# Picked rows of the second attention group through two PSUM banks in turn

## Chip, cores and metric

One core of one Trainium2 chip. The metric is device time in microseconds of one execution; before, three runs gave a median of 261.88 us (261.1 to 262.32).

## What is computed

Two blocks run one after the other on x of shape (2, 512, 128), both steered by a row of conditions. The first (quantised linear layers with a gated scan over time) is untouched and done before the stretch in question. The second begins with attention, 16 heads of width 8 over 512 positions:

```
xn = layernorm(x, g1, be1)
xm = xn * (1 + sc_a) + sh_a
qkv = xm @ Wqkv
scores = (q @ k.T) * 8 ** -0.5, causal
x = x + gt_a * (softmax(scores) @ v @ Wproj + bproj)
```

An MLP with its own normalisation follows.

## The kernel before, in words

The kernel is written engine by engine: five programs in a fixed order (PE, ACT, DVE, POOL, SP) that wait for each other by semaphores. PSUM is one tensor of eight banks, 128 by 512 fp32 each, called bank(0) to bank(7).

**Parts.** The scores are computed in bf16 from operands split into three bf16 parts. For each batch b and side i (0 for queries, 1 for keys) ACT writes `part[b][i][0]` (L739, a copy out of PSUM), DVE the remainder `rest` (L1216), ACT `part[b][i][1]` (L745), DVE `part[b][i][2]` (L1222, in `split_last`). The parts then go into stacks QS and KS, in which the six useful products of parts stand under each other.

**Stacks by DMA or by picking.** Attention runs in eight groups of four heads, four groups to a batch. Most heads are stacked by DMA: SP issues those of QS, POOL those of KS (`stack_parts`, L327). The first two groups of the first batch don't wait for DMAs: PE multiplies selection matrices (`picks`) with the three parts, which puts the stacked rows into a bank (`pick`, L1454, three matmuls with 512 columns), and ACT copies the bank into QS (L730) or KS (L732), in `picked`. The semaphore `picked_pe` counts the picks that PE has done, `picked_act` the copies of ACT. The first group is picked ahead of the attention into banks 4 to 7. The second group has four picks, low and side in turn: QS, KS, QS, KS. All four go through bank 6 and stand between the score items of the first group.

**Score items.** `S_ITEMS` cuts a group into 12 items by query tile and head, 256 to 512 columns wide. For each, PE makes three products (L1513 to L1515: scores and causal masks) in one of the banks 4, 5, 7 in turn, and DVE takes the row maximum (L1241). An item may start when DVE has read the item three before it (`bank_free`). After item 3 of the next group PE transposes the maxima (L1525), once POOL has split them into three bf16 parts (`split_maxima`, L474 to L480, which waits for all 12 items of its group). ACT copies them (L777), SP sends them into QS (L358), and PE computes the scores again for the exponentials, transposed and with the maxima as extra rows (`exp_slot`, L1553 to L1559, first behind item 7 of the second group). ACT takes the exponentials (L763), PE multiplies with V (L1573).

**Orders written out by hand around the change.** PE: projections of the second batch (L1463, L1469), items 0 to 2 of the first group, pick one, items 3 and 4, pick two, items 5 and 6, pick three, items 7 and 8, pick four, items 9 to 11, then the second group, whose first item waits for all six picked copies. Before each of the four picks PE waits until ACT has copied the previous one. ACT: part 0 of the second batch (L739), part 1 of it (L745, waits for DVE's remainders), the copy of V (L751), the four picked copies, then the maxima and exponentials. DVE: items 0 and 1, the remainders of the second batch (L1216, `split_rest`), items 2 to 5, its last parts (L1222, `split_last`), items 6 to 11 and on. POOL: the KS transfers of the second batch (ten for parts 0 and 1, two for part 2), two additions of a bias (L466), the splits of the maxima.

Of the kernel before, what the change touches and what calls it, by code (L numbers as in the profile page):

```python
# [84 lines left out]
NG = H // HG  # L85
HH = H // 2
PICKED = 2
HP = 2 * PICKED


# [51 lines left out]
def build(nc, x, cond_w, wa4, cond_rows, main_w, l1_w, bcast_rows, cols, rows1, consts, out):  # L142
    with ExitStack() as ctx:
# [43 lines left out]
        attn = [sb(f"attn{b}", [P, NT, D]) for b in range(B)]  # L187
        picks = sb("picks", [P, 2, 3, HP, P], BF16)

# [65 lines left out]
        S = {n: ctx.enter_context(nc.semaphore(n)) for n in SEMAPHORES}  # L255
# [62 lines left out]
        def stack_parts(queue, b, i, wanted=range(3)):  # L318

            stack, parts, done = ((QS[b], Q_PART, q_stacked[b]), (KS[b], K_PART, k_stacked[b]))[i]  # L320
            skip = HP if b == 0 else 0
            for want in wanted:
# [172 lines left out]
        def _(act):  # L495
# [146 lines left out]
            for i, parts in enumerate((Q_PART, K_PART)):  # L642
                for p in range(3):
                    slots = [s for s, q in enumerate(parts) if q == p]
                    step = slots[1] - slots[0] if len(slots) > 1 else 1
                    for half in range(2):
                        dst = picks[:, i, p, :, half * ROWS:(half + 1) * ROWS].rearrange("c h (s d) -> c h s d", d=HD)
                        src = ident_b[:, half * ROWS:half * ROWS + HP * HD].rearrange("c (d h) -> c h d", h=HP)
                        nc.scalar.activation(dst[:, :, slots[0]:slots[-1] + 1:step, :],
# [19 lines left out]
            def centre(b, n, done):  # L669

                act.wait_ge(S["ln_bias"], n)
                for t in range(b * NT, b * NT + NT):
                    ins = nc.scalar.activation(xhat[:, t, :], xs[:, t, :], ACT.Identity, bias=nbias[:, t:t + 1],  # L673
                                               scale=rstd[:, t:t + 1])
                ins.then_inc(done, 1)
# [50 lines left out]
            def picked(g, low, i, n, bk):  # L726

                act.wait_ge(S["picked_pe"], n)
                if i == 0:
                    ins = nc.scalar.activation(QS[0][:, slot_head(g, low), :], bank(bk), ACT.Copy)  # L730
                else:
                    ins = nc.scalar.activation(KS[0][:, slot_head(g, low), :], bank(bk), ACT.Identity,  # L732
                                               bias=k_f[:, KC["kone"][0]:KC["kone"][1]])
                ins.then_inc(S["picked_act"], 1)

            for b in range(B):
                for i in range(2):
                    act.wait_ge(S["qk_pe"], 2 * b + i + 1)
                    nc.scalar.activation(part[b][i][0][:, :], bank(2 + i), ACT.Copy,  # L739
                                         scale=QK_SCALE[i]).then_inc(S["part0"], 1)  # L740
                if b == 0:
                    centre(1, B + 1, S["xhat_ready"])
                for i in range(2):
                    act.wait_ge(S["rest_ready"], 2 * b + i + 1)
                    nc.scalar.activation(part[b][i][1][:, :], rest[b][i][:, :], ACT.Copy).then_inc(S["part1"], 1)  # L745
                if b == 0:
                    modulate_columns(1, 0)
                    picked(0, 0, 0, 1, 4)
                    picked(0, 1, 0, 3, 6)
                act.wait_ge(S["v_pe"], b + 1)  # L750
                nc.scalar.activation(V1[b][:, :, :, 0:HD].rearrange("p t h d -> p (t h) d"),  # L751
                                     bank(0).rearrange("p (n d) -> p n d", d=HD), ACT.Copy
                                     ).then_inc(S["v_ready"], 1)
            for n in range(4):
                low, i = divmod(n, 2)
                picked(1, low, i, 4 + n + 1, 6)

            def exp_slot(n, s):
                if s == 0 and n >= 2:
# [529 lines left out]
        def _(pe):  # L1289
# [45 lines left out]
            for i, j in enumerate((0, 1, 3, 4)):  # L1335
                ins = T.matmul(bank(4)[:, 16 + B * i:16 + B * (i + 1)], lw[:, a + j * D:a + (j + 1) * D], scT[:, :],
                               start=True, stop=True)
# [6 lines left out]
            for b in range(B):  # L1344
                ins = T.matmul(bank(4)[:, b:b + 1], crow[:, a + b * P:a + (b + 1) * P], cs_of(4, 7),
                               start=True, stop=True)
# [4 lines left out]
            for b in range(B):  # L1351
                for a in range(0, OUT6, 512):
                    z = min(a + 512, OUT6)
                    for c in range(OC):
                        ins = T.matmul(bank(2 * b + a // 512)[:, 0:z - a], cxq[:, c, b:b + 1].to_broadcast([P, P]),
                                       w4q[:, c, a:z], start=(c == 0), stop=(c == OC - 1))
# [4 lines left out]
            for i, j in enumerate((2, 5)):  # L1361
                for b in range(B):
# [3 lines left out]
                    ins = T.matmul(dst, ones[0:1, :], row1[:, g0 + i * D:g0 + (i + 1) * D], start=False, stop=True)  # L1366
# [44 lines left out]
            for t in range(NT):  # L1411
                for b in range(B):
# [5 lines left out]
                    for j in range(2):  # L1418
                        ins = T.matmul(bank(4 * b + 2 * (t % 2) + j), xq3[b][:, 1, tok(t)],
                                       weights("wm1")[:, j * MLP:(j + 1) * MLP], start=True, stop=True)  # L1420
# [30 lines left out]
            def pick(g, low, i, p, bk):  # L1451

                pe.wait_ge((S["part0"], S["part1"], S["part2"])[p], i + 1)
                return T.matmul(bank(bk), picks[:, i, p, slot_head(g, low), :], part[0][i][p][:, :],  # L1454
                                start=(p == 0), stop=(p == 2))
# [40 lines left out]
            def score_item(n, i):  # L1496
# [5 lines left out]
                bank_free(k)  # L1502
                if i == 0 and n < PICKED:
                    pe.wait_ge(S["picked_act"], (2, 6)[n])
# [30 lines left out]
            def exp_slot(n, s):  # L1535

                b, g = divmod(n, NG)
                use = 5 * n + s
                if use == 0:
                    pe.wait_ge(S["rest_ready"], 2 * B)  # L1540
                    pe.wait_ge(S["v_ready"], B)
                    pe.wait_ge(S["v_ones"], B)
                if s == 0:
                    pe.wait_ge(nm_stacked[n % 2], 32 * (n // 2 + 1))
                if use >= 2:
                    pe.wait_ge(S["p_ready"], use - 1)
                pairs = {0: [(0, 0)], 1: [(1, 0)], 2: [(0, 1), (0, 3)], 3: [(1, 1), (1, 3)], 4: [(0, 2), (1, 2)]}[s]
                for low, kt in pairs:
                    dsts = [bank(2 * (use % 2) + half)[:, p_at(2 * half + low, kt)[1] % L:][:, 0:L - kt * P] for half in range(2)]
                    h = slot_head(g, low)  # L1550
                    for half in range(2):
                        rows = half_rows(2 * half, XROWS)
                        T.matmul(dsts[half], KS[b][rows, h, tok(kt)], QS[b][rows, h, kt * P:L], start=True, stop=False)  # L1553
                    for half in range(2):
                        r = half_rows(2 * half)
                        T.matmul(dsts[half][:, 0:P // 2], k_of("pickLo", r), k_of("maskKlo", r), start=False, stop=False)  # L1556
                    for half in range(2):
                        r = half_rows(2 * half)
                        ins = T.matmul(dsts[half][:, 0:P], k_of("pickHi", r), k_of("maskKhi", r), start=False, stop=True)  # L1559
                ins.then_inc(S["st_pe"], 1)  # L1560
# [53 lines left out]
            for n in range(N_GROUPS + 3):  # L1614
                for i in range(len(S_ITEMS)):
                    if n < N_GROUPS:
                        score_item(n, i)
                    if n == 0 and i in (2, 4, 6, 8):
                        low, side = divmod(i // 2 - 1, 2)
                        pe.wait_ge(S["picked_act"], 2 + i // 2 - 1)  # L1620
                        for p in range(3):
                            ins = pick(1, low, side, p, 6)
                        ins.then_inc(S["picked_pe"], 1)
                    if i == MAXIMA_AT and 1 <= n <= N_GROUPS:
                        maxima(n - 1)
                    if i == MAXIMA_AT and n >= 3:
                        values_rows(n - 3)
                    if i in E_OLD and 2 <= n <= N_GROUPS + 1:
                        exp_slot(n - 2, E_OLD[i])
                    if i in E_NEW and 1 <= n <= N_GROUPS:  # L1630
                        exp_slot(n - 1, E_NEW[i])
                    if i in PV_AT and 2 <= n <= N_GROUPS + 1:
                        for kt in PV_AT[i]:
                            values(n - 2, kt)
                    if n == N_GROUPS and i == 7:
                        pe.wait_ge(S["nm_copied"], N_GROUPS)
                        columns_of_attention(0)
                if n == N_GROUPS:
                    projection(0)
                if n == N_GROUPS + 1:  # L1640
                    norm_columns(0)
# [6 lines left out]
            for t in range(NT):  # L1648
                for c in range(MLP // P):
                    ins = down(0, t, c, bank(W2_BANKS[0])[:, tok(t)])  # L1650
# [3 lines left out]
            for c in range(MLP // P):  # L1654
                for t in range(NT):
                    ins = down(1, t, c, bank(W2_BANKS[1] + t)[:, 0:D])
# [68 lines left out]
```

## Time and profile before

| | |
|---|---|
| median of 3 runs | 261.88 us |
| the profiled execution, its own time | 261.13 us |
| its span, first to last instruction | 259.3 us |
| mean granted TensorE clock | 0.841 |
| busy: PE, DVE, ACT, POOL | 154.9, 178.5, 152.4, 81.3 us |
| the four picks of the second group | from 151.42 to 159.9 us |
| first scores for exponentials | 167.56 us |

The span is what the profiler saw, and the execution's time has 1.8 us around it. Busy times are sums over the span and overlap each other. The attention starts near 150.6 us, the last group's items end near 222 us.

### The profile page before, as it was taken

How to read it: one execution, taken by the hardware profiler on the slowest of the kernel's cores; microseconds unless marked ns; L12 is line 12 of the kernel's file. 1: busy time of each engine (PE TensorE's matmuls, PEld its weight loads, DVE VectorE, ACT ScalarE, POOL GpSimd, SP SyncE). 2: the span in 40 equal slices, each digit the busy share in tenths (PEclk: the TensorE clock that was granted, in tenths of full speed). 3: DMA queues.
4: the chain of work that ended last, by engine and by line, in shares of the span. 5: the costliest groups of instructions: out<-in, count | busy, mean ns of one | idle time of the engine just before them, and what ended most of it. 6: DMA issues, size and time to landing. Idle time of an engine off the chain costs nothing.

```text
span 259.3 us, 4252 instructions
## 1 busy us (share of the span) xinstructions
PE 154.9 (60%) x1515; PEld 100.8 (39%) x1519; DVE 178.5 (69%) x483; ACT 152.4 (59%) x335; POOL 81.3 (31%) x120
## 2 busy tenths in 40 slices
PE   0221245915464130370638768699999999787985
PEld 0101133605352120210626343375566655354753
DVE  0778787999996976778576657687779877333411
ACT  3565669565796516596423753367568766885431
POOL 7234532332602513368311897111011101103110
PEclk9999999965755555586597997569999999999999
DMA  6996000000000000000000243033000000000011
GB/s 186 400 405 282 0 1 0 0 0 3 1 0 1 0 0 0 0 1 0 3 0 0 84 107 58 16 49 61 7 4 3 3 4 4 2 3 0 3 40 40
DMA packets 4490, 11.49 MB, mean 44 GB/s; under 512 B 1267, under 2 KB 2644, under 8 KB 3828
## 3 DMA queue, kind: packets, MB, share of 16 engines
q1 hardware_dynamic: 3510, 10.04, 11.3%
q0 software_dynamic: 960, 1.19, 2.0%
q8 instruction: 12, 0.20, 0.3%
q14 instruction: 8, 0.07, 0.1%
HBM read 8.24 MB, written 0.52 MB: 34 GB/s over the span
## 4 chain that ended last, share of the span: by engine, by line
DVE 39%; PE 33%; ACT 9%; POOL 7%; issue 6%; DMA 4%; SPq 1%; DVEq 0%; ACTq 0%
DVE negmax L1241 7%; PE ps L1573 5%; PE ps L1372 5%; POOL uh L448 4%; PE ps L1603 3%; PE ps L1609 3%; PE ps L1513 3%; DMA cw<-in_cond_w 2%; PE ps L1454 2%; DVE u L1047 2%; ACT xhat L673 2%; DVE mx L1133 2%; PE ps L1553 2%; DVE bnst L871 2%; DMA QS<-nmT 1%
## 5 line engine op out<-in xcount | busy, mean ns | idle before, releaser
L1241 DVE TENSOR_REDUCE negmax<-ps 128x1 f32<-128x384 f32 (+3 forms) x96 | 51.4, 595 | 15.7 <-PE ps L1515 15.6
L763 ACT ACTIVATE PT<-ps 128x1024 f32<-128x1024 f32 x40 | 39.6, 1033 | 20.7 <-PE ps L1559 20.6
L1513 PE MATMUL ps<-KS,QS 48*128 48x128 bf16 (+3 forms) x128 | 31.7, 324 | 1.0 <-DVE negmax L1241 0.7
L1372 PE MATMUL ps<-k_f,u 128*128 128x128 f32 x40 | 10.0, 425 | 32.9 <-ACT u L663 21.8
L1553 PE MATMUL ps<-QS,KS 51*128 51x512 bf16 (+3 forms) x128 | 24.8, 315 | 1.6 <-DMA QS<-nmT 1.6
L1514 PE MATMUL ps<-k_b 64*128 64x128 bf16 x128 | 24.1, 230 | 0.0
L381 POOL TENSOR_TENSOR rstd<-veps,mhalf 128x4 f32<-128x4 f32 x8 | 8.1, 1012 | 46.2 <-DVE veps L878 46.2
L1515 PE MATMUL ps<-k_b 64*128 64x64 bf16 x128 | 21.5, 197 | 0.0
L1372 PEld LDWEIGHTS ps<-k_f,u 128*128 128x128 f32 x40 | 7.6, 220 | 34.8 <-DVE u L1047 26.5
L1573 PE MATMUL ps<-PT,V 128*9 128x512 f32 (+3 forms) x256 | 20.0, 433 | 1.6 <-DVE attn L1251 1.6
L1559 PE MATMUL ps<-k_b 64*128 64x128 bf16 x128 | 18.7, 222 | 0.0
L474 POOL CAST nmpart<-negmax 128x16 bf16<-128x16 f32 x8 | 1.6, 197 | 53.4 <-DVE negmax L1241 53.4
L381 POOL TENSOR_TENSOR rms<-vms,mhalf 128x4 f32<-128x4 f32 x10 | 10.2, 1025 | 24.6 <-DVE vms L1021 24.5
L1556 PE MATMUL ps<-k_b 64*128 64x64 bf16 x128 | 17.7, 196 | 0.0
L1513 PEld LDWEIGHTS ps<-KS,QS 48*128 48x128 bf16 x128 | 11.0, 96 | 10.3 <-DVE negmax L1241 6.6
L327 POOL DMA_DIRECT2D KS<-part x24 | 13.4, 565 | 2.5 <-DVE part L1222 1.4
L1515 PEld LDWEIGHTS ps<-k_b 64*128 64x128 bf16 x128 | 12.0, 102 | 4.4 <-issue 0.8
L1302 PE MATMUL ps<-k_f,cq 2*128 2x2 f32 x14 | 2.3, 249 | 19.0 <-DVE cq L910 19.0
L1514 PEld LDWEIGHTS ps<-k_b 64*128 64x128 bf16 x128 | 11.5, 100 | 0.0
L448 POOL TENSOR_TENSOR uh<-prod,brow 128x512 f32<-128x512 f32 x8 | 9.8, 1266 | 5.3 <-DVE prod L1179 5.3
L1431 PE MATMUL ps<-k_f,uh 128*128 128x128 f32 x32 | 5.6, 350 | 9.7 <-DVE uh L1192 9.7
L1553 PEld LDWEIGHTS ps<-QS,KS 51*128 51x128 bf16 x128 | 9.3, 96 | 3.2 <-issue 2.1
(211 smaller groups left out, 462.8 us busy)
## 6 DMA issues: line engine op xcount, KB each, us to landing
w<-in_wa SPq DMA_DIRECT2D x2, 1152.0 KB, 10.7
lw<-in_l_w SPq DMA_DIRECT2D x1, 1280.0 KB
brow<-in_bcast_rows SPq DMA_DIRECT2D x1, 1152.0 KB, 16.0
mw<-in_main_w SPq DMA_DIRECT2D x1, 1024.0 KB, 13.5
KS<-part POOLq DMA_DIRECT2D x12, 64.0 KB, 3.7
QS<-part SPq DMA_DIRECT2D x12, 64.0 KB
cw<-in_cond_w SPq DMA_DIRECT2D x1, 576.0 KB, 5.6
xs<-in_x SPq DMA_DIRECT2D x1, 512.0 KB, 7.3
```

Of the source, the lines that this page charges most:

```text
L381: return nc.gpsimd.tensor_tensor(r, v, mhalf[0:v.shape[0], 0:v.shape[-1]], ALU.pow)
L448: nc.gpsimd.tensor_tensor(uh[b][:, t, :], prod[b][t % 2][:, :], brow_of("nm2"), ALU.mult).then_inc(S["uh_raw"], 1)
L763: nc.scalar.activation(PT[n % 2][:, s, :], bank(2 * (use % 2), 2), ACT.Exp).then_inc(S["p_ready"], 1)
L1241: V.tensor_reduce(negmax[n % 2][:, qt, h0:h0 + nh], bank(S_BANKS[k % 3])[:, 0:nh * w].rearrange("p (h w) -> p h w", w=w), AX.X, ALU.max, n ...
L1372: ins = T.transpose(dst[:, tok(t)], src(t), ident)
L1513: T.matmul(dst, QS[b][rows, h, tok(qt)], KS[b][rows, h, 0:w], start=True, stop=False)
L1514: T.matmul(dst[:, w - P:w], k_of("pickLo", r), k_of("maskQlo", r), start=False, stop=False)
L1515: ins = T.matmul(dst[:, w - P // 2:w], k_of("pickHi", r), k_of("maskQhi", r), start=False, stop=True)
L1553: T.matmul(dsts[half], KS[b][rows, h, tok(kt)], QS[b][rows, h, kt * P:L], start=True, stop=False)
L1556: T.matmul(dsts[half][:, 0:P // 2], k_of("pickLo", r), k_of("maskKlo", r), start=False, stop=False)
L1559: ins = T.matmul(dsts[half][:, 0:P], k_of("pickHi", r), k_of("maskKhi", r), start=False, stop=True)
L1573: ins = T.matmul(bank(6)[32 * j:32 * j + HD + 1, kt * P:L], V1[b][:, kt, g * HG + j, :], src, start=(kt == 0), stop=(kt == 2))
```

## The change

The four picks alternate between banks 6 and 1. The first two wait for no copy, the last two for the copy two picks before. ACT copies the first picked row between part 0 and part 1 of the second batch, the other three behind part 1 and ahead of the copy of V. The first scores for exponentials, which use banks 0 and 1, now also wait for all six picked copies. No instruction that computes is added or removed.

```diff
+PICK_BANKS = (6, 1)
+PICK_AT = (2, 4, 6, 8)
...
+            def picked_second(v):
+                low, i = divmod(v, 2)
+                picked(1, low, i, 4 + v + 1, PICK_BANKS[v % 2])
+
             for b in range(B):
...
                 if b == 0:
                     centre(1, B + 1, S["xhat_ready"])
+                if b == 1:
+                    picked_second(0)
                 for i in range(2):
                     act.wait_ge(S["rest_ready"], 2 * b + i + 1)
                     nc.scalar.activation(part[b][i][1][:, :], rest[b][i][:, :], ACT.Copy).then_inc(S["part1"], 1)
...
                     picked(0, 1, 0, 3, 6)
+                else:
+                    for v in range(1, 4):
+                        picked_second(v)
                 act.wait_ge(S["v_pe"], b + 1)
                 nc.scalar.activation(V1[b][:, :, :, 0:HD].rearrange("p t h d -> p (t h) d"),
...
-            for n in range(4):
-                low, i = divmod(n, 2)
-                picked(1, low, i, 4 + n + 1, 6)
...
                 if use == 0:
+                    pe.wait_ge(S["picked_act"], 6)
                     pe.wait_ge(S["rest_ready"], 2 * B)
...
-                    if n == 0 and i in (2, 4, 6, 8):
-                        low, side = divmod(i // 2 - 1, 2)
-                        pe.wait_ge(S["picked_act"], 2 + i // 2 - 1)
+                    if n == 0 and i in PICK_AT:
+                        v = PICK_AT.index(i)
+                        low, side = divmod(v, 2)
+                        if v >= 2:
+                            pe.wait_ge(S["picked_act"], 2 + v - 1)
                         for p in range(3):
-                            ins = pick(1, low, side, p, 6)
+                            ins = pick(1, low, side, p, PICK_BANKS[v % 2])
                         ins.then_inc(S["picked_pe"], 1)
```

## Rows read from the trace of the kernel before

**Rows 1.** Page of the profile, part 4: shares of the span by engine

```profile
DVE 39%; PE 33%; ACT 9%; POOL 7%; issue 6%; DMA 4%; SPq 1%; DVEq 0%; ACTq 0%
```

**Rows 2.** Chain of waits, 141 to 184 us: start, length, what ran

```profile
153.74 0.48 ACT V L751
154.23 0.50 ACT QS L730
...
154.99 0.61 PE ps L1454 x2
...
155.63 0.70 ACT KS L732
...
158.54 1.36 PE ps L1454 x3
...
160.35 1.90 DVE negmax L1241 x3
...
163.50 0.60 PE ps L1525 x4
...
165.53 1.89 DMA QS<-nmT
...
167.56 0.61 PE ps L1553 x2
```

**Rows 3.** Timeline of PE: start, length, instruction; in brackets the idle time before

```profile
151.42 0.82 PE L1454 MATMUL ps<-part,picks 128*128 128x512 bf16 x3
...
154.99 0.59 PE L1454 MATMUL ps<-part,picks 128*128 128x512 bf16 x2 [2.21 <-ACT QS L730]
```

**Rows 4.** Timeline of ACT

```profile
152.51 1.23 ACT L745 ACTIVATE part<-rest 128x512 bf16<-128x512 f32 x2 [2.07 <-DVE rest L1216]
```

**Rows 5.** Timeline of DVE

```profile
145.15 1.29 DVE L1222 TENSOR_TENSOR part<-rest,part 128x512 bf16<-128x512 f32 x2 [1.04 <-ACT part L745]
...
153.00 1.74 DVE L1241 TENSOR_REDUCE negmax<-ps 128x2 f32<-128x512 f32 x3
155.98 0.56 DVE L1241 TENSOR_REDUCE negmax<-ps 128x1 f32<-128x384 f32 x1 [1.24 <-PE ps L1515]
156.45 1.28 DVE L1222 TENSOR_TENSOR part<-rest,part 128x512 bf16<-128x512 f32 x2
```

**Rows 6.** Timeline of POOL

```profile
144.95 1.61 POOL L327 DMA_DIRECT2D KS<-part  x3
...
151.03 5.56 POOL L327 DMA_DIRECT2D KS<-part  x10 [0.50 <-issue]
158.03 1.12 POOL L327 DMA_DIRECT2D KS<-part  x2 [1.44 <-DVE part L1222]
159.17 2.49 POOL L466 TENSOR_TENSOR xs<-xs,bproj_g 128x512 f32<-128x512 f32 x2
162.30 0.20 POOL L474 CAST nmpart<-negmax 128x16 bf16<-128x16 f32 x1 [0.65 <-DVE negmax L1241]
```

**Rows 7.** Chain of waits over the whole span, two later groups

```profile
181.57 0.38 PE ps L1525 x4
...
189.99 0.38 PE ps L1525 x4
```

**Rows 8.** Stretches: length; busy us of PE, PEld, DVE, ACT, POOL; clock; DMA

```profile
152.80:156.20 3.40, 0.96 (x8) 0.44 (x9) 2.16 (x5) 2.48 (x5) 3.40 (x7) 1.00 0.54 123
156.40:159.60 3.20, 3.20 (x12) 0.94 (x12) 2.95 (x6) 0.60 (x1) 1.75 (x4) 0.50 0.45 72
159.80:163.00 3.20, 2.44 (x33) 1.67 (x33) 2.65 (x6) 0.69 (x1) 2.40 (x5) 1.00 0.06 18
163.20:167.50 4.30, 2.48 (x16) 1.37 (x16) 2.94 (x6) 1.87 (x2) 0.16 (x1) 0.50 0.01 3
167.50:173.20 5.70, 5.64 (x73) 4.25 (x74) 3.54 (x7) 3.77 (x4) 0.83 (x4) 0.50 0.45 72
173.40:181.80 8.40, 7.86 (x136) 4.97 (x133) 6.75 (x14) 5.88 (x8) 0.83 (x4) 1.00 0.30 49
```

## Prediction

> **What bounds the kernel now.** I read the page's chain shares first: no engine owns the span, DVE has 39% of the chain and PE 33% [rows 1]. So a stall is worth what it holds up in its own stretch. Next comes the chain in order of time around the picks [rows 2]: between 153.7 and 160.3 us it runs ACT, PE, ACT, PE, one behind the other, through the copy of V, the copy of a picked row, the next three picks, the next copy. That is one bank being filled, emptied and filled again. Then it leaves by the row maxima, POOL's split of them, the transposes, a transfer, and the first exponentials' scores at 167.56.
>
> PE's timeline shows the sharpest piece [rows 3]: the first three picks of the second group end at 152.24, and the next wait 2.21 us for the ACT copy at L730. ACT's timeline says why [rows 4]: ACT idles 2.07 us in front of the two L745 copies, which stand in its program ahead of the picked copy. DVE's timeline shows who suffers [rows 5]: after item 4 DVE idles 1.24 us for item 5, and its split of the last remainder (L1222) follows only at 156.45. On POOL [rows 6] the last two KS transfers wait for that split, the two bias additions follow, and the maxima's split begins at 162.30, when the twelfth reduction is done.
>
> About 0.5% (1.3 us) is what a measurement of this kernel can tell from no change.
>
> **The change, step by step.** Times are those of the profiled execution before; where I move an instruction I keep its duration.
>
> *First pick's copy.* Its picks still end at 152.24. The copy may start at about 152.27 instead of 154.23, 1.96 us earlier, and takes 0.50 to the next start [rows 2, 3]. The two part1 copies follow it: 152.77 to 154.00 instead of 152.51 to 153.74, so 0.26 later. They are waited for by DVE's L1222 and by POOL's transfers. L1222 comes after 155, and POOL is still issuing earlier transfers until 156.59 [rows 6], so this costs nothing. Without that cover it would be 0.26.
>
> *Second pick.* It goes to bank 1 and waits for no copy: behind items 3 and 4 PE is free at 154.99 − 2.21 = 152.78, and three picks take 0.82 [rows 3], so they end at 153.60. The 2.21 us go. Their copy, of 0.70 [rows 2], runs at 154.00 to 154.70. Bank 1 was last read by ACT's modulation for the second batch, before the projections that PE has already run, so nothing is late there.
>
> *Item 5 and DVE.* What is late next is DVE. It reduces items 2, 3 and 4 from 153.00 on [rows 5]. A 512-wide reduction takes 1.90/3 = 0.63 to the next start [rows 2], a 384-wide one 156.45 − 155.98 = 0.47. Item 5 needs the bank of item 2, free near 153.6, and is ready at about 154.0. So its reduction starts at 153.00 + 0.63 + 0.63 + 0.47 = 154.73 instead of 155.98: 1.25 earlier, not 2.21. L1222 follows 0.47 later as before, at 155.20, and ends 1.28 later at 156.48 instead of 157.73.
>
> *POOL.* Its ten earlier issues end at 156.59. Before, the last two began 0.30 after L1222's end; now that is 156.78. They take 1.12, the additions 2.49 [rows 6]: POOL is free at 156.78 + 1.12 + 0.02 + 2.49 = 160.41 instead of 161.66.
>
> *DVE up to item 11.* Item 6 comes a little before L1222's end, at 156.4, 7 at 156.9, 8 at 157.3, item 9 at 158.0, and items 9 to 11 take 1.90 as now: the end is 159.9. PE feeds them: picks three at 154.6 to 155.4, item 8 ready at 156.1, picks four until 156.9 (their bank's copies are over at 152.9 and 154.7), item 9 ready at 157.4, against DVE's 158.0. So DVE is done 0.5 before POOL, and POOL becomes the last one: L474 starts at about 160.42 instead of 162.30, **1.88 us earlier**. The gain is the 1.25 that DVE's chain gains and the 0.64 that POOL's queue had spare before.
>
> *From there on.* Split of the maxima, transposes, transfer (1.89) and scores [rows 2] have the same steps, so the scores start at 165.68. Later groups repeat at 189.99 − 181.57 = 8.42 us [rows 7] and hang on these, so I let the shift stand to the end. The transfers of the second batch are needed four groups later and cost nothing. The remaining copies end near 157.6, and V's second copy, moved behind them, near 158.2: 7 us before scores that wait for them, so the moved copy and the new wait at L1540 cost nothing. If that cover were gone they would cost the 0.48 to 0.70 of a copy.
>
> *Bounds.* From one side: if the chain of the picks alone set the time, all 2.21 us would go, and the excess of the picks at the low clock (1.36 instead of 0.82, twice, so 1.1) with them, 3.3 in all, though DVE's pace forbids it. From the other side: what the trace of before does not show is L1222 beside these very POOL issues. If they ran one after the other, POOL would lose up to L1222's 1.28, of which 156.78 − 156.59 is waiting anyway, so 1.1, and the gain would be 0.8. A loss on top needs the clock, below.
>
> *One rule against it.* The trace has the pairing once already, for the first batch: L1222 at 145.15 to 146.44 [rows 5], with POOL's issues at 144.95 taking 1.61 for three, 0.54 each, against 5.56 for ten, 0.56 each, later [rows 6]. This is the nearest row, the same two instructions, so I take the full 1.88. The Trainium skill (SBUF — State Buffer, Who interferes with whom) says that a DVE instruction with two SBUF inputs contends with a GpSimd instruction that reads SBUF. By that rule the gain would be the 0.8 and the time 261.1; the trace does not agree for these issues.
>
> **Sum.** 261.13 (profiled execution) − 1.88 = 259.25. That execution lies 0.75 under the median of 261.88, so against the median: **260.0 us**, 0.7% faster.
>
> **Rivals.**
> - *The clock gives more.* The granted clock is 1.2 GHz (0.50) from 156.4 to 159.6 and from 163.2 to 173.2, and 2.4 GHz (1.00) before, between and after [rows 8]. It fell the first time after PE had stood still for the copy, the second time after PE had been held by DVE's reductions from bank to bank. Without the stall the first fall should vanish, and the second may come and end earlier against the work. The scores after the transfer run in full PE use at half clock: 5.64 busy of 5.70. DVE idles 5.70 − 3.54 = 2.16 in it, and some of that stays, since its first item comes late. My estimate is that a third, 0.7, can be had, and two thirds, 1.4, at best. Time: 260.0 − 0.7 = 259.3, at best 258.6. Against it: the later low stretch begins with the DVE-paced items, which stay, and the transfer's idle time, which stays too.
> - *The gain is taken up on POOL or DVE.* If POOL's issues do get slower beside L1222, or DVE's reductions wait for each other, L474 starts 0.6 to 1.3 us later than I say: gain 0.6 to 1.3, time 260.6 to 261.3. For it: POOL is the last to arrive and its margin was 0.64. Against it: the 0.54 us issues.
> - *The change doesn't do what it says:* PE still stalls, because item 5 or 6 waits for DVE anyway and only idles elsewhere; time 261.9. Against it: DVE's own 1.24 us idle.
> - *Slower: the low clock lasts into the next group.* PE would be paced by DVE from about 157 on, 3 us earlier than now, and then idle for the transfer. If the clock came down with that and did not return until the second group was done, the 8.40 us in which PE is busy 7.86 [rows 8] would do about half their work: each us at half clock costs 0.47. It decides from 1.9/0.47 = 4 us more than now; a whole group costs 3.95, net 261.88 − 1.88 + 3.95 = 263.95. The Trainium skill (TensorE: Matmul & The Clock Gate, A second HAM failure mode: psum-queue depth-cycling) tells of a kernel whose turns through PSUM banks left PE idling briefly and its clock swinging. The fall at 163.2 after the DVE-paced items agrees with that; the return at 173.3 in full use speaks against so long a stay.
>
> **Chances.** My forecast (gain 1.4 to 2.4) 0.48, the clock gives more 0.17, the gain partly taken up 0.24, no effect 0.05, slower by the clock 0.06. Faster by over 0.5% needs 1.31: the first two, and a little of the third: 0.67. Within 0.5%: 0.27. Slower by over 0.5%: 0.06. The range leaves out the last case and most of no effect, and keeps the clock's best end: 258.6 to 261.4.
>
> **What would show it.** Right: no PE idle time of 2 us before L1454, item 5's reduction near 154.7, L1222 near 155.2, POOL's L466 followed at once by L474 near 160.4, first scores (L1553) near 165.7, clock 1.00 through the picks. Wrong: POOL's ten issues taking over 5.7 us, L474 released by DVE, or the clock back later than 6 us after the first scores.

## The result, and the profile after

The changed kernel takes 260.27 us (median of 18 runs, 258.26 to 260.8) against 261.81 for the kernel before in runs beside it (18 runs, 260.27 to 263.57). The ratio is 0.9934, with a 95% interval of 0.9914 to 0.9955, that is 1.2 to 2.3 us less. The forecast was 260.0 (258.6 to 261.4), faster. The profiled execution took 260.23, with a span of 258.4.

I measure the stretch that the change touches from the first score item (L1521 now, L1513 before) to the first scores for exponentials (L1562 now, L1553 before). Before it is 150.63 to 167.56, 16.93 us; after, 151.70 to 166.59, 14.89. It got 2.04 us shorter. The first items, by PE's timeline before and, in the second fence, after:

```profile
150.63 0.23 PE L1513 MATMUL ps<-KS,QS 48*128 48x128 bf16 x1
```

```profile
151.70 0.23 PE L1521 MATMUL ps<-KS,QS 48*128 48x128 bf16 x1
```

The profiled executions' times differ by 0.90 only, since the first item comes 1.07 later after. The delay arises ahead of the changed instructions: the first batch's projections ran at the low clock (0.50) and took 3.79 us, where they took 1.98 in the execution before. PE's timeline before, then the chain of waits after:

```profile
140.00 1.98 PE L1463 MATMUL ps<-xmT,lw 128*128 128x512 f32 x4 [0.93 <-ACT xmT L714]
```

```profile
139.72 3.79 PE ps L1471 x4
```

Both durations occur with the old picks and with the new ones: another execution of the changed kernel has 1.98, and a run of the kernel before, with only POOL's additions moved, has 3.78. Over all profiles here, 3 of 4 with the old picks have the short one, and 2 of 10 with the new picks. Whether the change makes the long one likelier stays open.

For a comparison with [rows 2 to 6] take 1.07 off the times that follow. PE's timeline after shows the four groups of three picks (L1462) and the waits beside them:

```profile
152.49 0.82 PE L1462 MATMUL ps<-part,picks 128*128 128x512 bf16 x3
...
153.78 0.82 PE L1462 MATMUL ps<-part,picks 128*128 128x512 bf16 x3
154.80 0.33 PE L1521 MATMUL ps<-KS,QS 48*128 48x384 bf16 x1 [0.20 <-DVE negmax L1249]
...
155.40 0.33 PE L1521 MATMUL ps<-KS,QS 48*128 48x384 bf16 x1 [0.18 <-DVE negmax L1249]
...
155.75 0.82 PE L1462 MATMUL ps<-part,picks 128*128 128x512 bf16 x3
...
156.92 0.82 PE L1462 MATMUL ps<-part,picks 128*128 128x512 bf16 x3
158.00 0.39 PE L1521 MATMUL ps<-KS,QS 48*128 48x512 bf16 x1 [0.25 <-DVE negmax L1249]
```

The 2.21 us of [rows 3] are gone. The second picks start right behind items 3 and 4, all picks take 0.82, and what PE waits for is now DVE's reductions, 0.18 to 0.25 at a time. ACT's timeline has the first copy ahead of the two part1 copies and the other three behind them:

```profile
153.35 0.60 ACT L732 ACTIVATE QS<-ps 128x512 bf16<-128x512 f32 x1 [1.83 <-PE ps L1462]
153.84 1.14 ACT L753 ACTIVATE part<-rest 128x512 bf16<-128x512 f32 x2
154.88 0.68 ACT L734 ACTIVATE KS<-ps,k_f 128x512 bf16<-128x512 f32 x1
156.61 0.60 ACT L732 ACTIVATE QS<-ps 128x512 bf16<-128x512 f32 x1 [1.05 <-PE ps L1462]
157.78 0.69 ACT L734 ACTIVATE KS<-ps,k_f 128x512 bf16<-128x512 f32 x1 [0.57 <-PE ps L1462]
158.37 0.59 ACT L762 ACTIVATE V<-ps 128x512 f32<-128x512 f32 x1
```

DVE's timeline no longer has the 1.24 us of idle time of [rows 5]. Four reductions (items 2 to 5) run together, then L1230 (L1222 before), then ten more without a gap:

```profile
154.06 2.21 DVE L1249 TENSOR_REDUCE negmax<-ps 128x2 f32<-128x512 f32 x4
156.19 1.28 DVE L1230 TENSOR_TENSOR part<-rest,part 128x512 bf16<-128x512 f32 x2
157.39 5.35 DVE L1249 TENSOR_REDUCE negmax<-ps 128x1 f32<-128x384 f32 x10
```

POOL's timeline shows what ends last now. The twelve KS transfers run through without the wait of [rows 6], the additions and the split (L476, L474 before) follow at once, and no bracket names another engine:

```profile
152.11 6.78 POOL L329 DMA_DIRECT2D KS<-part  x12 [0.24 <-issue]
158.90 2.49 POOL L468 TENSOR_TENSOR xs<-xs,bproj_g 128x512 f32<-128x512 f32 x2
161.33 0.20 POOL L476 CAST nmpart<-negmax 128x16 bf16<-128x16 f32 x1
```

The chain of waits agrees. Where [rows 2] had ACT, PE and DVE in turn, it now follows POOL's queue, from the split back to the transfers (and on, through those of the first batch):

```profile
152.11 5.58 POOL KS L329 x10
...
158.90 2.49 POOL xs L468 x2
...
162.54 0.60 PE ps L1533 x4
...
164.57 1.89 DMA QS<-nmT
...
166.59 0.61 PE ps L1562 x2
```

The clock, by stretches (columns as in [rows 8]), is full through the picks, and low from about 162 to 172:

```profile
153.80:157.80 4.00, 3.57 (x24) 1.31 (x21) 4.00 (x8) 2.37 (x6) 3.92 (x8) 1.00 0.49 121
157.80:161.80 4.00, 3.23 (x33) 1.93 (x33) 4.00 (x9) 1.16 (x2) 3.90 (x6) 1.00 0.44 64
162.40:166.50 4.10, 2.41 (x16) 1.18 (x16) 2.29 (x5) 1.87 (x2) 0.00 (x0) 0.50 0.01 3
166.50:171.90 5.40, 5.31 (x71) 4.06 (x72) 3.24 (x6) 3.44 (x4) 0.84 (x4) 0.50 0.47 76
```

### The profile page after: what moved, and what is told of

The parts are those of the page before. It is cut to its first block, busy times and chain, and to the rows that moved or that the text cites. A ratio compares the mean times of both kernels' runs of the same rounds, so it can differ in the third digit from the quotient of the medians.

```text
span 258.4 us, 4254 instructions
## 1 busy us (share of the span) xinstructions
PE 159.4 (62%) x1519; PEld 102.8 (40%) x1519; DVE 178.4 (69%) x483; ACT 152.0 (59%) x335; POOL 81.5 (32%) x120
## 4 chain that ended last, share of the span: by engine, by line
DVE 37%; PE 33%; POOL 14%; ACT 6%; issue 5%; DMA 3%; SPq 1%; DVEq 0%; POOLq 0%; ACTq 0%
DVE negmax L1249 7%; PE ps L1582 6%; POOL KS L329 5%; PE ps L1380 5%; POOL uh L450 4%; PE ps L1612 3%; PE ps L1618 3%; DMA cw<-in_cond_w 2%; PE ps L1521 2%; PE ps L1439 2%; DVE u L1055 2%; PE ps L1562 2%; PE ps L1363 1%; PE ps L1471 1%; DVE bnst L879 1%
## 5 line engine op out<-in xcount | busy, mean ns | idle before, releaser
L1249 DVE TENSOR_REDUCE negmax<-ps 128x1 f32<-128x384 f32 (+3 forms) x96 | 51.1, 594 | 14.0 <-PE ps L1523 13.8
L1521 PE MATMUL ps<-KS,QS 48*128 48x128 bf16 (+3 forms) x128 | 32.1, 321 | 1.4 <-DVE negmax L1249 0.8
L1562 PE MATMUL ps<-QS,KS 51*128 51x512 bf16 (+3 forms) x128 | 24.7, 315 | 1.6 <-DMA QS<-nmT 1.6
L476 POOL CAST nmpart<-negmax 128x16 bf16<-128x16 f32 x8 | 1.6, 199 | 52.8 <-DVE negmax L1249 52.8
L1521 PEld LDWEIGHTS ps<-KS,QS 48*128 48x128 bf16 x128 | 11.1, 96 | 10.6 <-DVE negmax L1249 7.9
L1439 PE MATMUL ps<-k_f,uh 128*128 128x128 f32 x32 | 6.4, 386 | 9.5 <-DVE uh L1200 9.5
L1562 PEld LDWEIGHTS ps<-QS,KS 51*128 51x128 bf16 x128 | 9.3, 96 | 3.2 <-issue 2.1
```

The lines of the kernel that those rows point to most:

```text
L1249: V.tensor_reduce(negmax[n % 2][:, qt, h0:h0 + nh], bank(S_BANKS[k % 3])[:, 0:nh * w].rearrange("p (h w) -> p h w", w=w), AX.X, ALU.max, n ...
L1521: T.matmul(dst, QS[b][rows, h, tok(qt)], KS[b][rows, h, 0:w], start=True, stop=False)
```

## The experiments

Every run is also read by the stretch above, from one profile each. That reading leaves out what came earlier in an execution: the changed kernel has 14.89 us with the first item at 151.70 and, in another execution, at 149.90.

### Either part alone

The order of ACT's copies alone, with one bank, and the wait for the previous copy back in front of each pick:

```diff
-PICK_BANKS = (6, 1)
+PICK_BANKS = (6, 6)
...
-                        if v >= 2:
-                            pe.wait_ge(S["picked_act"], 2 + v - 1)
+                        pe.wait_ge(S["picked_act"], 2 + v)
```

> The order of ACT's copies alone: all four picks stay in one bank and each waits for the copy of the one before. The measure is the stretch from the first score item to the first scores for exponentials: 150.63 to 167.56 = 16.93 us before, 151.70 to 166.59 = 14.89 us after the change. Theory A (what held the old order was the place of the first copy behind the two part1 copies, and one bank is enough once it is copied early): the second picks wait about 0.1 us instead of 2.2, the fourth some 0.4 us longer than with two banks, both hidden by DVE's pace; stretch 14.9, time as with the change, 260.2 (260.0 to 260.6). Theory B (two banks are what brings it): PE still waits about 0.6 us before each of the later picks and DVE waits for its items; stretch 15.6 or more, time 261 or more.

Measured: stretch 14.90 us, time 259.72 (ratio 0.991, 0.9879 to 0.9942). PE's timeline shows one wait for a copy, of 0.27 us ahead of the fourth picks, and it ends at 157.33, before DVE asks for the items behind it:

```profile
157.33 0.82 PE L1462 MATMUL ps<-part,picks 128*128 128x512 bf16 x3 [0.27 <-ACT QS L732]
```

The two banks alone, with ACT's copies where they were, behind the copy of V:

```diff
-                if b == 1:
-                    picked_second(0)
...
-                else:
-                    for v in range(1, 4):
-                        picked_second(v)
...
+            for v in range(4):
+                picked_second(v)
```

> The two banks alone: ACT copies the four picked rows where it did before, behind the copy of V. Theory A (either part alone takes PE out of the wait): second picks without a wait, third ones wait for the first copy until about 154.75 on the clock of before, which is when item 6 gets its bank anyway; stretch from the first score item to the first scores for exponentials 14.9, time 260.2. Theory B (the early copy is what brings it): the third picks wait for the late copy, items 7 and 8 are late for DVE by over 0.5 us, stretch 15.5 or more, time 260.9 or more.

Measured: stretch 14.89, time 259.34 (ratio 0.9893, 0.9857 to 0.9929). PE's timeline shows no wait for a copy ahead of the second or the third picks:

```profile
154.00 0.82 PE L1460 MATMUL ps<-part,picks 128*128 128x512 bf16 x3
...
156.05 0.82 PE L1460 MATMUL ps<-part,picks 128*128 128x512 bf16 x3
```

So theory A holds in both: what mattered was that PE's second picks need not wait for a copy that stands behind the part1 copies, and either part does that. The three versions' intervals overlap, so none is shown to be the faster one.

### What ends last now

The bias additions on POOL moved behind the first split of the maxima, in the changed kernel:

```diff
-            for b in range(B):
-                nc.gpsimd.tensor_tensor(xs[:, tiles(b), :], xs[:, tiles(b), :], over_tiles(bproj_g[:, b, :]), ALU.add
-                                        ).then_inc(S["biased"], 1)
...
             for n in range(N_GROUPS):
                 split_maxima(n)
+                if n == 0:
+                    for b in range(B):
+                        nc.gpsimd.tensor_tensor(xs[:, tiles(b), :], xs[:, tiles(b), :], over_tiles(bproj_g[:, b, :]), ALU.add
+                                                ).then_inc(S["biased"], 1)
```

> The changed kernel with POOL's two bias additions (2.49 us) moved behind the first split of the maxima. Theory A (POOL's queue is what ends last now, with DVE 0.4 us ahead of it): the first split starts about 0.4 us earlier and is released by DVE; stretch 14.45 instead of 14.89, time 259.8 (259.5 to 260.2), which is less than these rounds can tell from the changed kernel. Theory B (DVE's reductions are the bound and POOL just keeps pace): stretch 14.9, time 260.3.

Measured: stretch 14.51, time 259.23 (ratio to before 0.99, 0.9861 to 0.9938). POOL's timeline has the split now released by DVE after 2.08 us of idle time, 9.26 us after the first item instead of 9.63:

```profile
160.28 0.20 POOL L473 CAST nmpart<-negmax 128x16 bf16<-128x16 f32 x1 [2.08 <-DVE negmax L1250]
```

Theory A, by the profile: POOL's queue was the bound, and DVE was done 0.37 us before it (I had said 0.4). As expected, the times can't tell this version from the changed kernel.

The same move in the kernel before (same diff, other line numbers):

> The kernel before with only the two bias additions moved behind the first split of the maxima. Theory A (before, POOL had 0.64 us to spare and the split waited for DVE): stretch 16.93 as before, time 261.8 (261.5 to 262.1). Theory B (POOL's additions hold up DVE or the transfers): the stretch falls by 0.4 us or more.

Measured: time 261.69 against 261.76 (ratio 0.9981, 0.9946 to 1.0016), no difference that these runs can tell; the interval also holds the 0.4 us of theory B, so it doesn't decide. The stretch in its profile was 15.65, not 16.93, and most of that lies in the clock. PE waited as before (1.99 us for the copy at L731), but in this execution the clock stayed up and the third and fourth picks took 0.82. PE's timeline and two stretches of it:

```profile
156.13 0.82 PE L1455 MATMUL ps<-part,picks 128*128 128x512 bf16 x3 [1.99 <-ACT QS L731]
...
157.73 0.82 PE L1455 MATMUL ps<-part,picks 128*128 128x512 bf16 x3 [0.42 <-ACT KS L733]
...
159.24 0.82 PE L1455 MATMUL ps<-part,picks 128*128 128x512 bf16 x3 [0.27 <-ACT QS L731]
```

```profile
154.00:156.10 2.10, 0.14 (x6) 0.00 (x0) 2.10 (x4) 2.08 (x4) 2.10 (x5) 1.00 0.47 118
156.10:160.00 3.90, 3.18 (x22) 1.15 (x22) 2.66 (x7) 1.28 (x2) 2.47 (x6) 1.00 0.48 92
```

### The clock

First, the kernel before with PE kept busy in the stall by products that nothing uses:

```diff
+                        if i == 4:
+                            for _ in range(9):
+                                T.matmul(bank(1), picks[:, 0, 0, 0, :], part[0][0][0][:, :], start=True, stop=True)
                         pe.wait_ge(S["picked_act"], 2 + i // 2 - 1)
```

> The kernel before, with nine extra 512-column products on PE into the idle bank 1, ahead of the wait for the first copy (their results are used by nothing). It keeps the stall and takes away PE's idling. Theory A (the clock's first fall follows the stall, and it costs the third and fourth picks 0.5 us each): granted clock 1.00 from 156 to 160, those picks 0.8 us instead of 1.4, the split of the maxima 0.6 us earlier, when POOL is free, stretch 16.3, time 261.2. Theory B (the clock falls by itself there, whatever PE did in the stall): clock 0.50, stretch 16.9 or more, time 261.8.

Measured: stretch 16.04, clock 1.00 until past the split, picks of 0.82. That the products kept the clock up is not shown by this one profile, since it stayed up without them in the run above. Item 5's reduction was as late as ever (1.24 us of idle time on DVE). POOL's timeline has the additions followed at once by the split, 10.98 us after the first item instead of 11.67: POOL's 0.64 us of spare time was the limit, as expected. The run above, at the same clock and without the additions in front, had the split at 10.59, released by DVE. So the additions had time to spare only where the clock fell.

```profile
156.12 0.56 DVE L1241 TENSOR_REDUCE negmax<-ps 128x1 f32<-128x384 f32 x1 [1.24 <-PE ps L1515]
```

```profile
159.31 2.49 POOL L466 TENSOR_TENSOR xs<-xs,bproj_g 128x512 f32<-128x512 f32 x2
161.75 0.19 POOL L474 CAST nmpart<-negmax 128x16 bf16<-128x16 f32 x1
```

The median is 261.35 (ratio 0.9982, 0.9954 to 1.0009), no gain that these runs can tell. The profiles show two possible reasons. The kernel before perhaps doesn't always pay for the fall, as the run above suggests. And in the profiled execution the later low stretch lasted until about 177, 10.1 us after the first scores where it was 5.8 before, and the next group took 9.97 us instead of 8.42. The row of that stretch:

```profile
166.80:176.50 9.70, 9.69 (x105) 5.98 (x109) 6.20 (x11) 5.71 (x6) 0.84 (x4) 0.50 0.27 44
```

Another execution of the kernel before, unchanged:

> The kernel before, unchanged, in another execution. Theory A (whether the clock falls after the stall differs from execution to execution, as the run with only the later additions showed full clock there): the stretch from the first score item to the first scores is either 16.9 (clock 0.50 in the third and fourth picks) or 16.0 (clock 1.00, split of the maxima released by POOL). Theory B (the fall always follows the stall): 16.9.

Measured: 16.84. Here the clock fell, and the third and fourth picks took 1.46 and 1.31 us:

```profile
154.64 0.82 PE L1454 MATMUL ps<-part,picks 128*128 128x512 bf16 x3 [1.99 <-ACT QS L730]
...
156.24 1.46 PE L1454 MATMUL ps<-part,picks 128*128 128x512 bf16 x3 [0.42 <-ACT KS L732]
...
158.39 1.31 PE L1454 MATMUL ps<-part,picks 128*128 128x512 bf16 x3
```

So of three profiles with the old picks and nothing added on PE, the clock fell during the picks in two. In the nine profiles with the new picks whose clock is full during them, it fell in none before they were over, in the earliest case 2.9 us after the last. That agrees with the stall as the cause of the first fall, and doesn't prove it. Another execution of the changed kernel:

> The changed kernel, unchanged, in another execution. Both theories: stretch 14.9 whatever the clock does, since POOL's queue sets it; picks at full clock. What may differ is where the low clock ends after the first scores: 5.8 us after them as before, or some us earlier or later.

Measured: 14.89 again, time 257.94 in a single run. Its low stretch began near 159 and ended about 4.3 us after the first scores; the second group's maxima came 5.12 us after them instead of 5.59.

Second, the low stretch that stays. In the changed kernel, products that nothing uses: one behind each of nine items that DVE paces, three behind item 3 of the second group, and eight ahead of the first scores:

```diff
                         score_item(n, i)
+                    fill = {(0, 9): 1, (0, 10): 1, (0, 11): 1, (1, 0): 1, (1, 1): 1, (1, 2): 1, (1, 3): 3,
+                            (1, 4): 1, (1, 5): 1, (1, 6): 1, (1, 7): 8}.get((n, i), 0)
+                    if fill:
+                        pe.wait_ge(S["rest_ready"], 2 * B)
+                    for _ in range(fill):
+                        T.matmul(bank(2), picks[:, 0, 0, 0, :], part[0][0][0][:, :], start=True, stop=True)
```

> The changed kernel, with twenty extra 512-column products on PE between item 9 of the first group and the first scores for exponentials, where DVE paces PE or PE idles for the transfer (results used by nothing). Theory A (the second low stretch of the clock follows that idling, and the rival that the clock has more to give is right as to size): granted clock 1.00 at the first scores, the second group's maxima transposed some 0.7 us earlier after the first scores (6.05 us after them in the changed kernel), time 259.5 (258.9 to 260.0). Theory B (the clock falls anyway): the extra products run at half clock, 0.43 us each, the eight before the first scores delay them by up to 1.9 us, time 261 to 262.

Measured: clock 1.00 throughout the stretch and the next group, and the maxima 4.57 us after the first scores instead of 5.59, 1.0 us less. But the first scores came 16.51 us after the first item, 1.6 later than in the changed kernel: the items now followed PE's pace, and the eight products stood in front of the scores.

```profile
166.31 1.90 PE L1632 MATMUL ps<-part,picks 128*128 128x512 bf16 x8
```

```profile
163.60:168.10 4.50, 4.50 (x28) 2.02 (x27) 2.29 (x5) 1.87 (x2) 0.00 (x0) 1.00 0.06 17
168.10:172.70 4.60, 3.99 (x73) 2.82 (x73) 3.74 (x7) 3.86 (x4) 0.83 (x4) 1.00 0.50 75
```

Time 260.61 (ratio 0.9964, 0.9929 to 0.9999): no better than the changed kernel. Both theories were half right: the clock has the microsecond to give, and this way of asking costs more.

### Moving DVE's part away as well

DVE's last remainders of the second batch moved to item 7 of the second group, where DVE idles for the transfer, on top of the later additions:

```diff
-                    if n == 0 and i == 5:
+                    if n == 1 and i == 7:
                         split_last(1)
...
-                stack_parts(pool, b, 1)
+                stack_parts(pool, b, 1, range(3 - b))
...
                 if n == 0:
                     for b in range(B):
...
+                    stack_parts(pool, 1, 1, (2,))
```

> As the run with the later additions, and also DVE's last remainders of the second batch (L1222 of before, two of 0.64 us) moved behind item 7 of the second group, where DVE idles for the first scores, with POOL's two transfers of them behind the additions. Theory A (with POOL out of the way DVE's work up to item 11 is the bound, until PE's picks are): the first split starts some 1.1 us earlier than in the changed kernel; stretch 13.8 instead of 14.89, time 259.1 (258.7 to 259.6). Theory B (the picks and score items on PE already set the pace): stretch 14.4 as with the later additions alone.

> The run with the later additions and the later last remainders once more, for a profile at the full clock (the one taken showed a granted clock of 0.85 at best) and more timed runs. Theory A: the first split starts about 8.6 us after the first score item (9.63 in the changed kernel, 9.27 with the later additions alone), stretch to the first scores 13.8 us, time 258.6 to 259.2. Theory B (PE's items and picks hold it at the pace of the later additions alone): stretch 14.5, time 259.3 or more.

Measured, twice the same kernel: 258.56 (ratio 0.9885, 0.9847 to 0.9924) and 258.38 (0.9868, 0.9826 to 0.9909). In the second profile the split starts 8.54 us after the first item and the stretch is 13.61, against 8.6 and 13.8 expected; in the first, at a granted clock of 0.85 at best, they are 8.71 and 13.98. DVE's and POOL's timelines from the second:

```profile
153.70 2.67 DVE L1251 TENSOR_REDUCE negmax<-ps 128x2 f32<-128x512 f32 x5
156.60 5.06 DVE L1251 TENSOR_REDUCE negmax<-ps 128x1 f32<-128x384 f32 x9 [0.23 <-PE ps L1525]
...
163.81 1.28 DVE L1232 TENSOR_TENSOR part<-rest,part 128x512 bf16<-128x512 f32 x2
```

```profile
159.88 0.20 POOL L473 CAST nmpart<-negmax 128x16 bf16<-128x16 f32 x1 [2.58 <-DVE negmax L1251]
...
165.39 1.14 POOL L329 DMA_DIRECT2D KS<-part  x2 [2.01 <-DVE part L1232]
```

The five reductions, and after 0.23 us the next nine, run without L1232 (L1222 before) between them; it runs at 163.81, where it holds up nothing. This version is faster than the kernel before, and its stretch is 1.28 us shorter than the changed kernel's. That it also beats the changed kernel in time is not settled: of its two intervals one overlaps the changed kernel's, 0.9914 to 0.9955, and one lies below it by 0.0005, each with its own runs of the kernel before beside it, and the two banks alone, with the changed kernel's stretch, reached 0.9893.

The filling together with these moves:

> The later additions, the later last remainders and the extra products together. Theory A: the gains add, 1.1 us from POOL and DVE and 0.7 from the clock, time 258.4 (257.8 to 259.2). Theory B (the extra products sit in the way of score items once DVE and POOL no longer pace them): no better than the run with the later additions and last remainders, 259.1 or more.

Measured: 260.32 (ratio 0.9945, 0.9922 to 0.9967), stretch 16.19: theory B. Last, a lighter filling of the same kernel, one product of 128 columns behind each of nine items and four of 512 ahead of the first scores:

> The same with light filling of PE: one 128-column product behind each item of the DVE-paced stretch instead of a 512-column one (nine in all), none ahead of the transposes, and four of 512 columns instead of eight ahead of the first scores. Theory A (the loss in the filled run came from the size of the products, the clock's gain of 0.98 us stands): first scores no later than without filling, granted clock 1.00 there, maxima of the second group transposed 4.6 us after the first scores instead of 5.58, time 257.8 (257.2 to 258.6). Theory B (light filling doesn't keep the clock up): clock 0.50 at the first scores, which come up to 0.9 us later behind the four products, time 259 to 260.

Measured: 259.97 (ratio 0.9913, 0.9878 to 0.9948), stretch 15.31. In the profiled execution the clock fell all the same, and the four products, at half clock, stood in front of the first scores for 1.82 us. That is theory B:

```profile
162.00:167.10 5.10, 5.10 (x23) 1.93 (x20) 3.91 (x7) 1.87 (x2) 1.87 (x2) 0.50 0.10 28
```

Two of the twelve executions took 256.94 and 257.54 us, which is among the three lowest times of all, at a mean granted clock of 0.858 and 0.859, where the other ten had 258.68 to 260.9 at 0.846 to 0.855. They have no trace, so whether the light filling kept the clock up in them stays open.

## Why the prediction was right

*First pick's copy and part1.* Forecast 152.27, 152.77 and an end of part1 at 154.00; measured, with 1.07 off, 152.28, 152.77 and 153.91.

*Second pick, item 5, L1222.* Forecast picks from 152.78 on, measured 152.71. Forecast L1222 at 155.20, measured 155.12. DVE's gain is thus 1.33 us where I had 1.25, for the reason given: DVE, not PE, is late next. One reading was off: the 2.21 us of idle time in [rows 3] stand before two matmuls (x2) where a pick has three, so the record of the first is missing and the wait was some 0.2 us shorter, as the 1.99 in the other execution shows. Only the upper bound of 3.3 used it.

*POOL.* Forecast the split at 160.42, measured 160.26. The step with the miss is the 0.30 us that I kept between L1222's end and the last two transfers: POOL now reaches them with their part ready, and waits 0.08. They start at 156.69 where I had 156.78, some 0.1 of the 0.16 between 2.04 and my 1.88. That POOL becomes the bound by about half a microsecond is shown by the later additions (0.37).

*L1222 beside POOL's transfers.* Twelve issues took 6.78 us, 0.57 each, with L1230 running beside them at 156.19, against 0.56 for ten without it [rows 6]. The contention that bounded the gain at 0.8 did not come. The rule that I set against it need not cover these issues. The Trainium skill (SBUF — State Buffer, Who interferes with whom) has a DVE instruction with two SBUF inputs contend with a GpSimd instruction that reads SBUF, and the same section tells of a probe in which `tensor_copy` stalled DMA and `tensor_tensor`, the operation of L1222, did not. The 0.57 us agree with that.

*The shift to the end.* The later groups repeat at 8.34 to 8.56 us, most at 8.42, in every profile whose clock is full there, and from the first scores to the end of the span it is 91.7 us before and 91.8 after. So the stretch's gain does pass through.

*The sum.* I worked against one profiled execution, in which the clock had fallen after the stall, and took all picks at the full clock afterwards, so my 1.88 had the end of that fall in it. Against that execution's stretch the gain is 2.04. Where the clock doesn't fall, POOL ends last, and the kernel before would have about 16.0 us, as in the filled run, against 14.89 in both profiles of the changed kernel: a gain of 1.1. No profile of the unchanged kernel before shows that case. The medians' 1.54 lies between, but that this is the reason is not shown, since executions also differ outside the stretch: the first item came 1.07 us later in the one profiled after, and two executions of the changed kernel with the same stretch took 260.23 and 257.94. So my 1.88 was right as a difference of two stretches, for the reasons given, and somewhat high against the medians, though inside the measured 1.2 to 2.3. That the forecast came within 0.3 us of 260.27 is partly luck.

*The rivals.* That the clock gives more: its first fall is gone, worth 0.9 of the 2.04 where it came, by the filled run. The second stayed, 5.59 us from scores to maxima against 5.58 before, and the 0.7 to 1.4 that I put on it was the right size, 1.0 in the filled version of the changed kernel. The slower rival's mechanism exists: in the filled kernel before, the low stretch lasted 4.3 us longer and cost the group 1.55, some 0.36 us each where I had put 0.47. It did not come in the two profiles of the changed kernel, whose clock was back 5.8 and 4.3 us after the first scores. That the gain is taken up on POOL is refuted as to its cause.

## What to carry to other kernels

Before giving a stalled producer a second buffer, look where its consumer's copy stands in the consumer's program: here moving one copy forward, or a second bank alone, did what both together did. After a stall goes, follow each engine's own queue to the next meeting point and write down when each arrives; the one that is last there (POOL's queue, with DVE done 0.37 us before it) is where the next gain lies, and moving work with a late due time off both took another 1.28 us from the stretch. Work against more than one profiled execution where the clock changes inside the stretch.

## What I had not expected of the hardware

The same wait of PE can bring the clock down or not: 1.99 us idle ahead of the second picks were followed by 0.50 in one execution of the kernel before (and much the same wait in that of [rows 8]), and by 1.00 in the run with only the later additions. The end of the later low stretch moves too: 5.8 and 4.3 us after the first scores in two executions of the changed kernel, 5.8 and 5.7 in two of the kernel before, 10.1 in the filled kernel before. The Trainium skill (TensorE: Matmul & The Clock Gate, What's actually happening) says that the clock's state follows how busy PE has been of late. The filled version of the changed kernel, which stayed at 1.00 with PE busy 4.50 of 4.50 us ahead of the scores, agrees; the filled kernel before, at 0.50 with PE busy 9.69 of 9.70 us, shows that full use doesn't always bring the clock back soon. What makes two executions of one program differ, no run here shows.
